# Reordered instruction sequences in the prologue and the last batch of a gated cross-attention and attention kernel

## The reference

```
x [4,512,512], ctx [4,512,512]
x = x + tanh(g_xattn) * einsum('emk,enk->emn', fp8_1x128(layernorm(x)), fp8_128x128(ctx))
h = layernorm(x)
fused = h @ (Wa * col_scale)      # Q,K: 16 heads x 24 std columns each, V: 512, Q_low,K_low: 16 x 8 each
q_tail, k_tail = (K_low, Q_low) where w_rec > 0.1 else (Q_low, K_low)
out = causal softmax(Q K^T / sqrt(32)) V
x = x + tanh(g_ffn) * (out @ Wp)
```

## Time and profile before

| | us |
|---|---|
| median of 3 runs | 501.77 |
| the runs | 500.73, 501.77, 505.46 |
| the profiled execution | 500.87 |
| its span | 499.1 |

### The profile page before, as it was taken

One profiled execution on the slowest core, in us unless ns is written; L12 is line 12 of the kernel. 1 busy time (PEld: TensorE's weight loads), 2 busy tenths in 40 slices (PEclk: granted clock), 3 DMA queues, 4 the chain that ended last, 5 costly groups with the idle time before them and its releaser, 6 DMA issues.

```text
span 499.1 us, 8044 instructions
## 1 busy us (share of the span) xinstructions
PE 443.6 (89%) x2600; PEld 317.4 (64%) x2600; DVE 333.3 (67%) x1093; ACT 257.2 (52%) x510; POOL 156.5 (31%) x282
## 2 busy tenths in 40 slices
PE   0468799998869999999769999999879999999996
PEld 0244577775536788776535788777545778676765
DVE  3899536879993254788997243788997236566733
ACT  1777446567445570558445463448655424363530
POOL 4988775343223300243213400144122100111110
PEclk9989999999979999999988999999998999999999
DMA  6412083324400345324410234514300144234112
GB/s 215 175 33 85 14 260 91 90 71 107 133 1 2 81 105 153 101 53 98 115 61 2 53 95 98 177 39 105 92 23 1 45 104 102 56 94 102 53 44 85
DMA packets 28217, 42.62 MB, mean 85 GB/s; under 512 B 8304, under 2 KB 8688, under 8 KB 28176
## 3 DMA queue, kind: packets, MB, share of 16 engines
q1 hardware_dynamic: 26752, 41.19, 29.7%
q10 hardware_dynamic: 1232, 0.54, 0.5%
q0 software_dynamic: 192, 0.39, 0.3%
HBM read 12.59 MB, written 4.19 MB: 34 GB/s over the span
## 4 chain that ended last, share of the span: by engine, by line
PE 69%; DVE 16%; POOL 5%; ACT 3%; issue 3%; DMA 2%; SPq 0%; POOLq 0%; DVEq 0%; ACTq 0%
PE pv_bank L788 14%; PE mm_bank L613 9%; PE mm_bank L614 8%; PE mm_bank L615 8%; DVE x_all L1261 6%; PE max_bank L757 6%; PE exp_bank L774 6%; DVE max_bank L1293 3%; PE mm_bank L815 2%; PE mm_bank L817 2%; PE mm_bank L816 2%; PE turn_bank L629 2%; PE pv_bank L797 2%; ACT work L1036 2%; DMA ctx_raw<-in_ctx 2%
## 5 line engine op out<-in xcount | busy, mean ns | idle before, releaser
L1293 DVE CUSTOM_DVE_ANT_0 max_bank<-max_bank,causal 128x512 f32<-128x512 f32 (+3 forms) x256 | 121.6, 509 | 58.1 <-PE max_bank L757 49.8
L1036 ACT ACTIVATE work<-exp_bank 128x512 f32<-128x512 f32 (+1 forms) x192 | 94.6, 528 | 89.9 <-PE exp_bank L774 88.8
L527 POOL TENSOR_SCALAR_AFFINE_SELECT work<-work 128x384 f32<-128x384 f32 x64 | 33.5, 524 | 280.6 <-ACT work L1036 280.6
L788 PE MATMUL pv_bank<-work,v_aug 128*33 128x256 f32 (+3 forms) x512 | 78.5, 449 | 0.8 <-POOL work L530 0.8
L757 PE MATMUL max_bank<-k_stack,q_stack 96*128 96x512 f32 x248 | 67.8, 338 | 5.4 <-DVE row_max L1293 5.4
L774 PE MATMUL exp_bank<-q_stack,k_stack 97*128 97x512 f32 (+3 forms) x256 | 69.1, 335 | 3.5 <-ACT work L1036 1.8
L1261 DVE SCALAR_TENSOR_TENSOR x_all<-mm_bank,coef,x_all 128x128 f32<-128x128 f32 x224 | 61.1, 341 | 0.2 <-issue 0.2
L788 PEld LDWEIGHTS pv_bank<-work,v_aug 128*33 128x33 f32 x512 | 28.4, 113 | 49.4 <-issue 40.0
L613 PE MATMUL mm_bank<-xt_hi,w_hi 128*128 128x512 f32 x128 | 54.1, 422 | 1.5 <-POOL w_lo L543 1.5
L774 PEld LDWEIGHTS exp_bank<-q_stack,k_stack 97*128 97x128 f32 x256 | 45.5, 189 | 14.9 <-ACT work L1036 4.8
L1276 DVE SCALAR_TENSOR_TENSOR qk_lo<-mm_bank,col_root,qk_hi 128x512 fp32r<-128x512 f32 x32 | 24.0, 748 | 44.8 <-ACT qk_hi L1007 44.8
(11 more groups left out here) (176 smaller groups left out, 810.8 us busy)
## 6 DMA issues: line engine op xcount, KB each, us to landing
q_stack<-qk_hi SPq DMA_DIRECT2D x128, 64.0 KB, 2.0
k_stack<-qk_hi SPq DMA_DIRECT2D x120, 64.0 KB, 2.0
ctx_raw<-in_ctx SPq DMA_DIRECT2D x16, 256.0 KB, 3.3
x_all<-in_x SPq DMA_DIRECT2D x16, 256.0 KB, 4.6
q_stack<-qk_lo SPq DMA_DIRECT2D x64, 64.0 KB, 2.0
out<-x_all SPq DMA_DIRECT2D x16, 256.0 KB, 2.5
k_stack<-qk_lo SPq DMA_DIRECT2D x60, 64.0 KB, 2.0
work<-in_L_ffn_Wa SPq DMA_DIRECT2D x3, 768.0 KB, 9.4
```

The costliest lines, as they stand in the source:

```text
L527: pool.affine_select(out=three, in_=three, compare_op=ALU.is_ge, fill=0.0, base=0, pattern=[[0, 3], [1, P]], channel_multiplier=-1)
L788: last = pe.matmul(pv_bank[64 * j:64 * j + D + 1, P * m:T], v_aug[:, m, 2 * u + j, :], prob[j][:, PROB_COL[m]:PROB_COL[m] + T - P * m], st ...
L1036: act.activation(prob[j][:, UNIT_COL[k]:UNIT_COL[k] + UNIT_LEN[k]], exp_bank[(3 * j + k) % 2][:, 0:UNIT_LEN[k]], ACT.Exp, scale=SCALE).the ...
L1293: last = dve.tensor_tensor_reduce(max_bank[unit % 2][:, col:col + width], max_bank[unit % 2][:, col:col + width], causal[:, T - width:T], ...
```

## The change

Nothing is added or removed in the prologue: the same pieces stand in another order on PE, ACT, DVE and POOL. In the last batch the order of side pieces between score pieces is another, too, and two pieces at the end of `DVE_LAST` (`Z1`, `z2`) move to the head of the end string. The code of the pieces and all their waits are as before; the twelve `w` of PE stay twelve, in other places.

```diff
 PE_LAST (steps 0 to 3 of 8)
-    "v3.0 rowmax max0 max1 Q2.01 max2 v3.1 max3 exp0 exp1 max4 Q2.2 exp2 v3.2 max5 exp3 v3.3 Q2.3 exp4 exp5",
-    "max0 K2.01 max1 rowmax K2.2 pv max2 exp0 exp1 max3 K2.3 exp2 back exp3 max4 exp4 Q3.0 max5 exp5 Q3.1",
-    "max0 rowmax Q3.2 max1 pv exp0 max2 exp1 Q3.3 max3 max4 exp2 exp3 K3.0 exp4 max5 back exp5",
-    "K3.1 rowmax K3.2 max0 max1 pv exp0 max2 max3 exp1 K3.3 exp2 z0 exp3 max4 max5 exp4 Y0 exp5 back",
+    "v3.0 rowmax max0 Q2.0 max1 Q2.1 v3.1 max2 exp0 Q2.2 max3 exp1 max4 v3.2 exp2 exp3 v3.3 exp4 max5 Q2.3 exp5 K2.0",
+    "K2.1 rowmax max0 max1 pv max2 exp0 K2.2 exp1 max3 K2.3 exp2 back exp3 max4 exp4 Q3.0 max5 exp5",
+    "Q3.1 max0 rowmax Q3.2 max1 pv exp0 max2 max3 exp1 Q3.3 exp2 K3.0 max4 max5 exp3 back exp4 K3.1 exp5",
+    "max0 rowmax K3.23 max1 pv exp0 max2 exp1 Y0 exp2 max3 exp3 back max4 exp4 z0 max5 exp5",
...
-PE_FIRST = ("f0 w0 w1 f1 w2 f2 f3 w3 w4 f4 w5 S0 S1 f5 S2 S3 f6 S4 w6 S5 S6 S7 w7 S8 "
-     "S9 S10 S11 w8 f7 S12 w9 f8 S13 w10 S14 f9 w11 S15 v0 v1.01 f10 v1.2 f11 v1.3 q0.0 B0 q0.123 k0.0 "
-     "B1 k0.123 V2 M0 M1 q1.01 M2 q1.23 k1.01 M3 k1.2 M4 k1.3 M5")
+PE_FIRST = ("f0 f1 w0 w1 f2 f3 w2 f4 w3 w4 S0 S1 w5 f5 S2 S3 f6 S4 S5 S6 S7 w6 w7 S8 "
+     "S9 S10 w8 S11 w9 w10 f7 S12 w11 S13 S14 f8 f9 S15 v0 v1.012 f10 f11 v1.3 q0.012 B0 q0.3 k0.0 B1 "
+     "k0.123 V2 M0 M1 q1 M2 k1.012 M3 M4 k1.3 M5")
-ACT_FIRST = ("d0 C0 a0 a1 C1 C2 C3 b0 C4 C5 f4 b1 C6 f5 s0 a2 f6 s1 C7 e3 b2 f7 a3 N0 "
-     "s2 N1 f8 f9 s3 b3 v0 N2 N3 f10 f11 v1 q0 p0 k0 c0 V2 D0 D1 q1 c1 c2 k1 c3")
+ACT_FIRST = ("d0 C0 C1 a0 C2 a1 b0 C3 C4 a2 C5 f4 C6 b1 f5 s0 a3 f6 b2 C7 s1 e3 f7 N0 "
+     "b3 N1 f8 s2 f9 s3 v0 N2 N3 f10 f11 q0 v1 k0 p0 c0 V2 D0 c1 q1 D1 c2 k1 c3")
-DVE_FIRST = ("t0 t1 t2 t3 w0 A0 A1 x0 x1 x2 x3 T0 L0 L1 F0 F1 G0 L2 L3 F2 f0 F3 f1 f2 "
-     "G1 T1 T2 c0 f3 T3 S0 S1 S2 S4 S5 S6 b0 S8 b1 S9 S10 S12 S13 h0 S14 u0 b2 b3 "
-     "h1 u1 u2 u3 h2 h3 B0 B1 q0 k0 M0 M1 M2 M3 q1 M4 M5 k1")
+DVE_FIRST = ("t0 t1 w0 t2 t3 A0 A1 x0 x1 x2 x3 T0 f0 L0 L1 F0 f1 L2 F1 G0 L3 F2 F3 G1 "
+     "f2 T1 f3 c0 T2 S0 S1 S2 S4 S5 S6 S8 S9 b0 S10 b1 T3 S12 S13 u0 h0 S14 h1 b2 "
+     "u1 b3 u2 u3 h2 h3 B0 B1 q0 k0 M0 M1 q1 M2 M3 M4 M5 k1")
-POOL_FIRST = ("s0 s1 i0 l0 s2 s3 s4 s5 s6 s7 j0 l1 j1 a0 l2 a1 r0 r1 l3 a2 j2 a3 r2 r3 "
-     "o0 j3 g0 g1 D0 g2 g3 D1 p0 v0")
+POOL_FIRST = ("s0 s1 i0 s2 s3 l0 s4 s5 s6 s7 l1 j0 l2 j1 a0 a1 l3 r0 r1 j2 a2 a3 r2 r3 "
+     "o0 j3 g0 g1 g2 D0 D1 g3 v0 p0")
...
 END_LAST
-    "DVE": "Z2 norm Z3 z3 Z8 Z9 Z10 Z11",
+    "DVE": "z2 Z1 Z2 norm Z3 z3 Z8 Z9 Z10 Z11",
```

## The result

| | before | after |
|---|---|---|
| median us (20 runs each) | 501.85 | 498.29 |
| lowest, highest | 497.14, 505.46 | 495.83, 502.97 |
| profiled execution, span | 500.87, 499.1 | 497.15, 495.4 |

The ratio of after to before is 0.9942, with a 95% interval of 0.9921 to 0.9963: the change takes 2.9 us off (1.9 to 4.0). The ratio is taken over fast runs, without the two of the kernel before that lie over 1.5% above its fastest (505.46 and 504.67), so it is not the quotient of the two medians (0.9929). The forecast was 499.7.

The account below looks back on a forecast made before the run. DVE and POOL were taken to bound the prologue, PE the last batch. Terms -1.85 (q0), +0.3 (q1) and 0 (last batch) gave -1.55: 499.3 on the profiled execution, 500.2 on the median, 499.7 said; 8-in-10 range 497.2 to 502.3.

Parts of the forecast that it names:

- The gate: Prologue: the first Q product on PE waits for POOL's fourth j (L543), 1.5 us before the change.
- Up to S0: DVE and POOL before the S additions: S0 starts at 32.4 instead of 36.1; POOL's s7 ends by 30.9.
- To a3: From S0 to POOL's last a: a3 starts at 49.7, not 51.73, held by ACT's s3.
- The term of q0: First Q product on PE: starts at 58.1, with unchanged 8.24 us behind a3; gain 1.85 us.
- q1: PE after the first Q product: q1 waits for ACT's V2 copy; loss 0.3 us, bounds 0 and 1.2.
- The last batch: PE full, same products, in 27 groups before and after: gain 0, bounds -0.5 to +0.5 us.
- The sum: Whole kernel: -1.85 + 0.3 + 0 = -1.55 us; 499.3 on the profiled execution, 499.7 said.
- A bound that doesn't add up: Prologue: if each piece of T1, T2, T3 ran alone (0.29), S0 would start 2.8 earlier; gain 2.2 us.
- The port: DVE and POOL share an exclusive SBUF lock; T3 in its new place waits some tenths instead of 1.3 us.
- No gain: T pieces meet POOL's long instructions again, or q1's wait takes 1.2: 500.9 to 501.8 us; chance 0.17.
- Large gain: POOL isn't the brake, DVE's 3.7 us pass almost whole: 497.7 on the profiled execution; chance 0.15.
- Slower by the clock: PE gaps before q0 and around v0 halve the clock, costing 3.4 us: 502.7; chance 0.08.

Follow-up runs that it names:

- T3 back: Changed kernel with the exchange T3 moved back in front of the first S addition on DVE; ratio 1.0006 to the kernel before.
- l0 back: Changed kernel with l0 on POOL moved back in front of s2 and s3; ratio 0.9942 to the kernel before.
- T3 beside j2: Changed kernel with T3 two S additions later, behind S13, where POOL is in j2; ratio 1.0011 to the kernel before.
- f0 and f1 back: Changed kernel with DVE's copies f0 and f1 of turned ctx back in their later places; ratio 0.9994 to the kernel before.
- T3 alone: Kernel before with only T3 moved behind S10, all other sequences old; ratio 0.9994 to the kernel before.

## Why the prediction was right, point by point

- **The gate.** Right for the new prologue by itself, where the first Q product waits 1.70 for L543 on POOL. In the first profile of the changed kernel the last `h` came 0.4 behind j3; v0 had run at half clock.
- **Up to S0.** Forecast S0 at 32.4, 19.6 after the first tile; measured 19.5 to 20.0. POOL's s7 at 18.1; measured 18.2 to 18.6. T2 2.1 (2.2), T3 1.0 (0.8).
- **To a3.** Forecast 36.9 after the first tile and held by ACT's s3; measured 37.1 (48.31 - 11.21) and held by ACT (0.58). The 8.24 from there to the first Q product were 8.27 in the kernel with only the prologue new (49.40 to 57.67), and 8.54 in the first profile of the changed one, where the last `h` came last. With these the first Q product was forecast at 45.3 after the first tile and came at 44.96, 45.38 and 45.64.
- **The term of q0.** Forecast 1.85; by the first Q product 2.20 (new prologue), 1.78 and 1.52 (changed). Right size. The old prologue scatters too: with 47.48 of the kernel with only the last batch new as the base, each is 0.3 more.
- **q1.** The wait of 0.3 was 0.33. But it is no loss in the sum: the first normalisation comes 37.71 after the first Q product in both kernels. Something in the new order wins back what the wait costs, perhaps that q1 is undivided and k1 in two runs instead of three; no kernel tried that by itself. With V2 moved away the surplus shows as 0.44 to 0.47.
- **The last batch.** Forecast 0; 0.04 in the trace, 0.9994 in the runs. The products stand in 28 groups before and 29 after, not 27 and 27; nothing hung on that.
- **The sum** was the mis-sized part: 1.55 forecast, 2.9 (1.9 to 4.0) measured. 1.55 lies below the interval. The 0.3 at q1 belongs out of it, and 2.2, the largest of the three values, fits the interval. Where the remaining 0.7 lies, if it is real, no row shows: the start of the first tile differs by 0.9 on average between the old and the new order, and from the first normalisation to the first of the last batch the profiles scatter by more (334.28 before, 332.42 to 334.59 in the three profiles of the new prologue). That 499.7 came so near to 498.29 is in part luck: it was set between the sums on the profiled execution (500.87) and on the median of three runs, and so stands 2.15 under the median of twenty runs, where the working gave 1.55.
- **A bound that doesn't add up.** With each piece of T1 and T2 at 0.29, S0 would be 2.3 earlier (1.9 and 2.1 less 0.87 each), not 2.8. The gain of 2.2 in that bound hung on POOL and not on this.
- **The port.** The forecast used the lock that the Trainium skill, "SBUF — State Buffer", section "SBUF: two separate sides", describes for VectorE instructions in a two-port mode or with two inputs in SBUF, and took a short wait for T3 beside r0. The rows of T3 back agree with the lock piece by piece. Beside r0's and r1's operations on 128x1, though, T3's pieces took 0.26, 0.30 and 0.30, as alone: there the measurement shows no wait at all. In the kernel with l0 back the copy of T3 runs from start to end inside one of them:

```profile
44.26 0.71 POOL L488 TENSOR_TENSOR rstd<-rstd,neg_half 128x1 f32<-128x1 f32 x1
44.67 0.26 DVE L1324 COPY x_all<-x_all 128x256 f32<-128x256 f32 x1
```

- **The rivals.** "No gain" is real, one step away: three of the four kernels with one piece of the new order put elsewhere (T3 back, T3 beside j2, f0 and f1 back) land at 0.9994 to 1.0011, and only l0 back keeps the gain. "Large gain" fails at the last `a`, as argued. "Slower by the clock" occurred in part: the clock did fall at v0, and cost 0.3 in the first profile of the changed kernel (45.64 against 45.38 in the second, the last `a` at 37.1 in both), as j3 hides most of the 1.2 by which the last `h` was later.

## What to carry to other kernels

Where VectorE copies in SBUF beside a busy GpSimd, read the end of each copy against GpSimd's instructions. Beside large ones (0.7 us and more here) three copies in a row ended behind three of them; beside operations on 128x1 they ran as alone. Look for a stretch in which GpSimd does tiny operations, and move the copies and GpSimd's pieces together; the copies moved without the rest (T3 alone) and the rest without the copies (T3 back) gave nothing here. Judge such a move by a start that both profiles share, since the loads before it scattered by 2.7 us.

## What the runs showed of the hardware

VectorE operations on 8 columns were held as long as big ones: G0's first scale took 0.53 instead of 0.17 beside l0 in the changed kernel, and a scale took 0.96 with f0 and f1 back. An operation on 16 columns took 0.97 instead of 0.23 beside the first GpSimd tile. The coefficients (128x64) took 1.03 beside a GpSimd tile against 0.21 with f0 and f1 back, where they found a gap. Small size doesn't protect an operation; small size of GpSimd's instruction beside it does.

In the gap between two GpSimd instructions of which the second waits for the first by a semaphore, a second VectorE piece slipped in (27.32, 0.29, between 27.24 and 27.34 in the changed kernel). Between GpSimd instructions without such a wait only one did. I saw this in every row that I read, but made no kernel for it alone.
